# Two row transfers in flight, weights split early and kept, eight shared tiles behind the routed ones, sums on two engines

## The reference

```python
x = x + _L0_ffn_ref(_L0_cond_ref(x, ...), W_fc, W_proj)      # cosine attention, then a spiking FFN
x = x + _L1_ffn_ref(_L1_cond_ref(x, fside, ...), g1, g2, ...)  # attention, then a block with experts
...
# _L0_ffn_ref: h = square(relu(x @ W_fc.T)); y = h @ W_proj.T; 5 spiking steps on y; mean of the spikes
# _L1_ffn_ref:
X = X + attention(_rmsnorm(X, g1))
xf = _rmsnorm(X, g2)
rw = softmax(xf @ Wr.T + expert_bias)
topw, topi = top_k(rw, 2); topw = softmax(topw)
shared = _swiglu(xf, sW1, sW2, sW3)            # silu(x @ w1.T) * (x @ w3.T) @ w2.T
specialist = sum over the two chosen experts of topw * _swiglu(xf, eW1[e], eW2[e], eW3[e])
return X + shared + specialist
```

## Time and profile before

| what | value |
|---|---|
| three runs | 1443.07, 1442.61, 1438.27 us; median 1442.61 |
| the profiled execution | 1443.43 us, of it 1441.70 span from first to last instruction |
| granted TensorE clock, mean | 0.954 of full |
| busy, share of the span | PE 91%, VectorE 72%, ACT 62%, GpSimd 49% |
| moved | 71.19 MB, mean 49 GB/s |

### The profile page before, as it was taken

The page is one execution under the profiler, slowest core; times in us unless marked ns, Lnnn a source line. Parts: engine busy times, 40 slices in busy tenths (PEclk is TensorE's granted clock), DMA queues, the critical chain, the costliest instruction groups (busy, mean ns, idle before and its releaser), DMA issues.

```text
span 1441.7 us, 42824 instructions
## 1 busy us (share of the span) xinstructions
PE 1307.1 (91%) x15311; PEld 1157.7 (80%) x15312; DVE 1037.4 (72%) x2148; ACT 897.6 (62%) x2309; POOL 708.2 (49%) x797
## 2 busy tenths in 40 slices
PE   4899999999689999889999999689999789999980
PEld 3799999998579999778888888668788678888870
DVE  4798988988736465687887887768987686555446
ACT  3677777777356666656666666478775354555545
POOL 2556555564435454545445444357777562333330
PEclk8899999999799999999999999899997999999995
DMA  8200000001030000000000000020012623333319
GB/s 230 54 8 10 8 9 9 8 11 37 3 87 1 1 0 1 3 9 10 8 9 9 9 9 12 23 56 16 16 29 72 211 80 111 105 104 101 101 44 349
DMA packets 87025, 71.19 MB, mean 49 GB/s; under 512 B 49981, under 2 KB 80831, under 8 KB 85824
## 3 DMA queue, kind: packets, MB, share of 16 engines
q1 hardware_dynamic: 80320, 51.73, 12.7%
q0 software_dynamic: 6528, 17.05, 3.3%
HBM read 39.47 MB, written 24.02 MB: 44 GB/s over the span
## 4 chain that ended last, share of the span: by engine, by line
PE 56%; issue 20%; POOL 10%; DVE 9%; ACT 3%; DMA 1%; another core or an unknown queue 0%; ACTq 0%; POOLq 0%; DVEq 0%; SPq 0%
PE psQ L2348 9%; PE psQ L1957 7%; PE psW L2035 7%; PE psW L2327 5%; POOL pn L759 5%; PE psQ L2148 3%; POOL rq L785 3%; PE psS L2148 3%; PE psW L2136 3%; PE psM L2136 3%; PE psS L2059 2%; PE psT L1986 2%; PE psT L2070 2%; PE psM L2009 2%; PE psT L2316 2%
## 5 line engine op out<-in xcount | busy, mean ns | idle before, releaser
L1957 PE MATMUL psQ<-xT,wq 128*128 128x256 f32 x1536 | 224.8, 298 | 3.5 <-ACT cur L1117 1.8
L2035 PE MATMUL psW<-wout,oT 128*128 128x256 f32 x1536 | 207.8, 294 | 1.1 <-ACT oT L980 1.1
L1957 PEld LDWEIGHTS psQ<-xT,wq 128*128 128x128 f32 x1536 | 205.0, 201 | 4.4 <-issue 2.6
L2035 PEld LDWEIGHTS psW<-wout,oT 128*128 128x128 f32 x1536 | 196.6, 199 | 1.3 <-ACT oT L980 1.3
L2348 PE MATMUL psQ<-W,exT 128*128 (+1 forms) x624 | 172.3, 412 | 0.0
L759 POOL TENSOR_TENSOR pn<-ex,rden 128x1024 f32<-128x1024 f32 x64 | 124.5, 1945 | 45.2 <-DVE rden L1440 45.2
L980 ACT ACTIVATE oT<-psT,small 128x512 fp32r<-128x512 f32 x128 | 81.1, 684 | 91.3 <-PE psT L2070 91.2
L915 POOL DMA_INDIRECT results<-result,idx x72 | 70.1, 974 | 135.3 <-ACT result L1244 131.9
L803 POOL TENSOR_TENSOR hT<-hf,hT 128x512 fp32r<-128x512 f32 x64 | 85.8, 1341 | 102.1 <-ACT hT L1113 102.0
L771 POOL TENSOR_TENSOR masked_bias<-bias_t,negmask 128x1024 f32<-128x1024 f32 x32 | 68.8, 2150 | 132.6 <-DVE ex L1408 132.6
L1367 DVE SCALAR_TENSOR_TENSOR oT<-psT,small,oT 128x512 fp32r<-128x512 f32 x128 | 90.2, 746 | 58.3 <-ACT oT L980 58.3
(11 more groups left out here) (302 smaller groups left out, 3391.6 us busy)
## 6 DMA issues: line engine op xcount, KB each, us to landing
rows<-sorted SPq DMA_DIRECT2D x72, 132.0 KB, 2.1
both<-results SPq DMA_DIRECT2D x8, 1024.0 KB, 13.7
raw_w<-W SPq DMA_DIRECT2D x27, 256.0 KB
vv<-vp SPq DMA_DIRECT2D x256, 16.0 KB, 1.8
out<-X SPq DMA_DIRECT2D x8, 512.0 KB, 8.8
X<-x SPq DMA_DIRECT2D x1, 3584.0 KB, 18.1
bvv<-v_all SPq DMA_DIRECT2D x128, 16.0 KB
sorted<-rows SPq DMA_DIRECT2D x9, 132.0 KB
```

Of the source, the lines that this page charges most:

```text
L1957: mm = nc.tensor.matmul(psQ[:, cc, h * QT:h * QT + QT], wq[w][:, k, c * P:c * P + P], xT[g % 2][u][:, k, :], start=(k == 0 and j == 0), st ...
L2035: mm = nc.tensor.matmul(psW[:, 0:D], oT[u][:, c, :], wout[w][:, c, :], start=(u == 0 and c == 0 and w == 0), stop=(u == 1 and c == CH - 1))
```

## The change

- `FIRST` becomes 24: steps 0 to 23 are shared tiles, 24 to 95 the 72 routed tiles, 96 to 103 the last eight shared tiles.
- The raw pieces of the experts' weights are loaded during the FFN into three small buffers, both parts are made there by VectorE (3 pieces behind group 0, 4 behind each of groups 1 to 6), and SP stores each of the 27 pieces to a buffer in device memory (`parked`), waits for the store to land and loads the next but two piece. ACT and VectorE wait for the last store before they reuse the memory at the attention's start. Later an expert's weights come in as one load of 1.5 MB, already split: expert 0 at the end of the second attention (SP waits until it landed), then 1; 2 at the end of the block; 3 to 8 when the block's rows are done. ACT and VectorE do no splitting in the expert steps.
- Each send of rows waits until the send two before it has landed (`x_sent0`, `x_sent1`); the wait on PE's transpositions goes. The batches are (0, 8), (8, 24), (24, 32), 16 sends stand in the block, and the choices are cut into shorter parts at other steps.
- The experts' weights of the sum are computed in steps 9 to 21. ACT scales the results of groups 0 to 4 and VectorE sums groups 0 and 2 in steps 103 to 107; groups 1, 3 and 5 are summed by GpSimd, the others by VectorE behind the last step.

```diff
-FIRST = TILES
+FIRST = 3 * TILES // 4
-BATCHES = ((0, 12), (12, 24), (24, TILES))
-FIRST_CHOICE, SECOND_CHOICE, PLACES = (-14, -2, 5), (-13, -1, 6), (-11, 1, 8)
-RANKED_BEFORE, RANK = (19, 31), 7
-SEND_STEP, SENT_IN_BLOCK = 26, 14
-ENDS, SLOTS, MARGINS = (10, 12, 14), (16, 18, 20, 22, 24), 26
+BATCHES = ((0, 8), (8, 24), (24, TILES))
+FIRST_CHOICE, SECOND_CHOICE, PLACES = ((-18, -17), (-2, -2), (5, 5)), ((-16, -15), (-1, -1), (6, 6)), ((-12, -11), (2, 2), (8, 8))
+RANKED_BEFORE, RANK = 17, {2: 1, 7: 2}
+SEND_STEP, SENT_IN_BLOCK, IN_FLIGHT = 26, 16, 2
+ENDS, SLOTS, WEIGHTS = (10, 11, 12), (13, 14, 15, 16, 17), (9, 18, 20, 22)
+POOL_GROUPS = (1, 3, 5)
+SCALE_STEP, SUM_STEP = {103: 0, 104: 1, 105: 2, 106: 3, 107: 4}, {104: 0, 106: 2}
...
-SPLIT_STEP = [-4, -3, -2, 0, 1, 2, 3, 4, 5] + list(range(10, 28))
+PARKED = [3] + [4] * (GROUPS - 2)
+PIECES = KD + 1
...
+            def load_piece(n):
+                p, part = divmod(n, PIECES)
+                raw = raw_piece[n % 3][:, 1, :]
+                got = sem(f"p_raw{n % 3}")
+                if part < KD:
+                    for j, w in enumerate(("W1", "W3")):
+                        sp.dma_start(raw[:, j * D:j * D + D], a[w][p, part * P:part * P + P, :]).then_inc(got, 16)
+                else:
+                    sp.dma_start(raw.rearrange("p (k n) -> p k n", k=KD), a["W2"][p].rearrange("(k p) n -> p k n", p=P)).then_inc(got, 16)
+            def park(n):
+                p, part = divmod(n, PIECES)
+                sp.wait_ge(sem("p_lo"), n + 1)
+                sp.dma_start(parked[p, :, :, part * 2 * D:part * 2 * D + 2 * D], piece[n % 3][:].bitcast(F32)).then_inc(sem("p_kept"), 16)
+                sp.wait_ge(sem("p_kept"), 16 * (n + 1))
+            for n in range(3):
+                load_piece(n)
+            for n in range(PIECES * EP):
+                park(n)
+                if n + 3 < PIECES * EP:
+                    load_piece(n + 3)
             spread_v(LAYERS[1], load_block)
             def load_expert(p, slot, done):
...
+                sp.dma_start(W[:, slot, :, :].bitcast(F32), parked[p]).then_inc(done, 16)
             sp.wait_ge(sem("t_oev"), 2 * TILES)
-            for p in range(2):
-                load_expert(p, SHARED_SLOT + p, sem("e_first"))
+            load_expert(0, SHARED_SLOT, sem("e_weights"))
+            sp.wait_ge(sem("e_weights"), 16)
+            load_expert(1, SHARED_SLOT + 1, sem("e_weights"))
...
-                if n >= SENT_IN_BLOCK and k == 0:
-                    pool.wait_ge(sem("e_xTp"), (t - SENT_IN_BLOCK // TOP_K) * 8 // 7 + 1)
+                reach(pool, sem(f"x_sent{n % IN_FLIGHT}"), 16 * (n // IN_FLIGHT))
                 send(t, k)
...
+            for n, g in enumerate(POOL_GROUPS):
+                x = X[:, G4 * g:G4 * g + G4, :]
+                pool.wait_ge(sem("y_scaled"), g + 1)
+                nc.gpsimd.tensor_tensor(x, x, both[g][:, :, 0, :], ALU.add).then_inc(sem("y_half"), 1)
+                pool.wait_ge(sem("y_half"), 2 * n + 1)
+                nc.gpsimd.tensor_tensor(x, x, both[g][:, :, 1, :], ALU.add).then_inc(sem("y_half"), 1)
...
+            def split_piece(n):
+                part = n % PIECES
+                hi, lo = piece[n % 3][:, 0, :], piece[n % 3][:, 1, :]
+                raw = raw_piece[n % 3][:, 1, :]
+                dve.wait_ge(sem(f"p_raw{n % 3}"), (0 if n % 3 else 16) + sum(16 if m % PIECES == KD else 32 for m in range(n % 3, n + 1, 3)))
+                if part < KD:
+                    then(nc.vector.tensor_scalar(hi, raw, g2col[:, part:part + 1], None, ALU.mult))
+                    ins = nc.vector.scalar_tensor_tensor(lo, raw, g2col[:, part:part + 1], hi.bitcast(F32), ALU.mult, ALU.subtract)
+                else:
+                    then(nc.vector.tensor_copy(hi, raw))
+                    ins = nc.vector.tensor_tensor(lo, raw, hi.bitcast(F32), ALU.subtract)
+                ins.then_inc(sem("p_lo"), 1)
             ffn_in_lo(0, 0)
...
+            for g in range(GROUPS):
+                ffn(g, g % 2, first=g == 0, last=g == GROUPS - 1)
+                if g < GROUPS - 1:
+                    for n in range(sum(PARKED[:g]), sum(PARKED[:g + 1])):
+                        split_piece(n)
...
                     if isinstance(t, int) and t in (0, FIRST):
-                        pe.wait_ge(sem("e_wlo"), 3 * EP if t else 3)
+                        pe.wait_ge(sem("e_weights"), 16 * EP if t else 16)
```

More of the change, by code:

```diff
@@ L336, in build @@
         count = sb("ffn_work", "count", [P, G4 * D], BF16)
+        pieces_at = (place["xT"][0] - 8 * K, place["ffn_work"][0])
+        piece = [nc.alloc_sbuf_tensor_at(f"piece{i}", [P, 2, 2 * D], F32R, offset=pieces_at[i // 2] + 4 * K * (i % 2)) for i in range(3)]
+        raw_piece = [nc.alloc_sbuf_tensor_at(f"raw_piece{i}", [P, 2, 2 * D], F32, offset=pieces_at[i // 2] + 4 * K * (i % 2)) for i in range(3)]
         place["ffn_work"][0] += 8 * K
@@ L646, in _ @@
             sp.wait_ge(sem("d_xf"), TILES)
[L647 to L650, removed]
+            for p in range(3, EP):
+                load_expert(p, (p + 1) % EP, sem("e_weights"))
             def row_number(table, n, last):
@@ L662, in _ @@
             sp.wait_ge(sem("blanked"), 16 * (E + 1))
-            sp.wait_ge(sem("x_sent"), 16 * TOP_K * TILES)
+            for n in range(IN_FLIGHT):
+                sp.wait_ge(sem(f"x_sent{n}"), 16 * TOP_K * TILES // IN_FLIGHT)
             for r in range(ROUTED):
@@ L677, in _ @@
             for g in range(GROUPS):
-                sp.wait_ge(sem("y_acc"), g + 1)
+                done = sum(h not in POOL_GROUPS for h in range(g + 1))
+                if g in POOL_GROUPS:
+                    sp.wait_ge(sem("y_half"), 2 * (g + 1 - done))
+                else:
+                    sp.wait_ge(sem("y_acc"), done)
                 sp.dma_start(out_dram[:, G4 * g:G4 * g + G4, :], X[:, G4 * g:G4 * g + G4, :]).then_inc(sem("stored"), 16)
@@ L1804, in read_ranks, with places @@
                 dve.wait_ge(sem("r_read"), b + 1)
-            def places(b):
+            def places(b, k):
                 tiles = slice(*BATCHES[b])
-                if b == 2:
+                if b and k == 0:
                     read_ranks(b)
-                for k in range(TOP_K):
-                    mine = rt[1 + k][:, tiles, :]
-                    then(nc.vector.tensor_tensor(mine, mine, place_of[:, tiles, :], ALU.mult))
-                    then(nc.vector.tensor_reduce(pos[:, k, tiles], mine, AX.X, ALU.add))
+                mine = rt[1 + k][:, tiles, :]
+                then(nc.vector.tensor_tensor(mine, mine, place_of[:, tiles, :], ALU.mult))
+                then(nc.vector.tensor_reduce(pos[:, k, tiles], mine, AX.X, ALU.add))
+                if k == 0:
+                    return
                 nc.vector.tensor_copy(row_place[:, :, tiles], pos[:, :, tiles]).then_inc(sem("r_placed"), 1)
@@ L1896, in first_half @@
                     tile_slots(SLOTS.index(i))
-                elif i == MARGINS:
+                elif i == WEIGHTS[0]:
                     margins()
-                for piece in range(3 * EP):
-                    if SPLIT_STEP[piece] == i:
-                        split_expert(piece // 3, piece % 3)
+                if i == WEIGHTS[2] - 1:
+                    top_weights()
+                elif i == WEIGHTS[3] - 1:
+                    late_weights()
             def merged(i):
```

179 lines of the change are left out of this document (77 added, 102 removed).

## The result

The changed kernel takes 1476.91 us (median of 4 runs, 1474.19 to 1479.59) against 1441.69 for the kernel before (4 runs, 1438.27 to 1443.07): a ratio of 1.0249, interval 1.0229 to 1.0268. It is slower, by 2.5%. The forecast was 1462, range 1428 to 1482.

What follows compares the result with a forecast made beforehand. PE was taken to bound the FFN, with gains possible only in the shared steps and tail. The sum was 1443.4 + 25 + 2.5 + 2 - 11.5 + 1 = 1462.4, so 1462 us, range 1428 to 1482.

Steps and rivals of the forecast that it cites:

- FFN, +25: FFN: the fourth piece's wait for its reloaded buffer idles PE 3.3 us a group plus 1.7 of clock, five times.
- The transition, +2.5: Behind FFN group 6: four more pieces ahead of the next attention's norm_first cost 2.5 us, ends 0 and 5.
- The block's start, +2: Block's start: SP waits for the first expert's 1.5 MB before spreading bvv, costing 2 us, ends 0 and 4.
- The shared steps, -13.5 before the clock: Shared expert steps: rows let the first routed tile start at 1196 instead of 1209.8; -11.5 after the clock.
- The tail, +1: After the last routed product: 38.3 us against 37.5, ended by ACT's scalings, GpSimd's sums beside them; ends -3 and +4.
- The routed steps: Routed steps: the clock behind PE's wait for rows was put at 2 us, taken off the shared steps' gain.
- B: FFN rival: store and load are quick, so the kernel is not slower; centre 1436 us, chance 0.28.
- C: Expert-step rival: 48 sends in a row hold PE up, 7.1 us a gap; 1472 us, chance 0.15.
- D: Expert-step rival: sends keep their share beside the weights, landing 2.6, 9 us less, 1453; a quarter of the forecast's share.

Runs made afterwards that it cites:

- experiment 1: Changed kernel with two of the four weight pieces behind groups 1 to 6 moved ahead of ffn_in_lo, where VectorE is idle: 1456.16 us, ratio 1.0087.
- experiment 6: The run with both, experts 3 to 8 loaded one at a time: 1464.8 us; the last run of experiment 4 without SP's early wait for expert 0: 1451.72.
- Experiment 3: Changed kernel with all 32 shared tiles ahead of the routed ones again: 1471.21 us, ratio 1.0223.
- experiment 4: All eight result sums on VectorE, none on GpSimd: in the changed kernel 1474.21 us, in the run with both 1451.37.
- experiment 2: Changed kernel with four row sends in flight instead of two: 1466.44 us; with no limit on sends: 1486.07 us.
- the last run of experiment 4: The run with both, with all eight sums on VectorE and none on GpSimd: 1451.37 us, ratio 1.0075.
- experiment 5: Kernel before with only the limit of two sends in flight, in place of the wait on PE's transpositions: 1446.89 us, ratio 1.0045.
- the run with both: Changed kernel with weight pieces moved to VectorE's idle time and all 32 shared tiles ahead of the routed ones: 1454.6 us, ratio 1.01.

## Why the prediction was right, and where its terms were off

The direction and the main reason held, and the time lay 15 us under the measured one. That it came so near is in part luck. In the profiled execution two terms came out 28 us too low (the shared steps with the routed ones 22.7, the tail 5.7), and 16 of that were taken back: by the FFN's 4.8, and by 11.1 in the stretches outside it and ahead of the expert steps, where 4.5 were forecast and -6.6 measured, most of that spread. By its own steps:

- **FFN, +25: right in mechanism, 5 us too large.** Measured +20.2 in the FFN, and 20.7 undone by experiment 1. The fourth piece waits 2.4 to 2.7 us in each of six groups, PE stands 2.2 instead of 3.3 (store 3.2 where I put 3.6, load 2.2 where I put 2.6 with its issue), and the clock, 0.94 over 30 us, takes 1.8 more, where I put 1.7. Choosing 3.6 between 2.1 and 7.7 by the straight loads was the right choice of row.
- **The transition, +2.5: nothing.** From the last ffn_in_lo to the first product of the attention it is 31.2 as against 31.4.
- **The block's start, +2: PE did wait 3.25 us, yet the block got no longer.** From the first projection to the first expert step it takes 163.4 as against 165.5; by experiment 6 the wait cost some 1.5 of them.
- **The shared steps, -13.5 before the clock: this is the step that failed.** I wrote that two in flight hold the sends up only where a landing takes longer than 2 x 1.28, and the landing I took, 2.4, was right to the digit (2.43). But the next send doesn't start when the one before the last lands: it starts 0.8 us later, by the chain above. A pair takes 2.43 + 0.8 = 3.23, not 2.56. And beside the weights a landing took 6.0 to 7.3, not 4.0, which was the end of my range. With these, 8 sends in the 29 us from 1138 to 1167 and 1.61 for each of the 37 behind it, the first routed tile stands 109 behind the first step, not 87. So a term forecast as a gain was a loss of 8.1.
- **The tail, +1: +6.7.** I let ACT's scalings end it. VectorE's sums do: they start 13.7 us behind the last routed result instead of 8.3, because of the shared steps, and each of VectorE's steps that meets a sum of GpSimd lasts as long as that. I had counted GpSimd's 16 us as lying beside the rest. Experiment 3 shows 3 of it as the price of the eight tiles, experiment 4 a further 2.8 as that of the division.
- **The routed steps** took 3.1 more. Of it 2 are the clock, as I had put: it is half while PE waits (0.53 from 1188 to 1231) and 0.61 from 1231.4 to 1236.4, and full from there on. The other 1.1 are open.

Of the rivals, B falls with the store's 3.2 and the load's 2.2. C named the right time for the wrong reason: 48 sends in a row did come, but with two in flight no gap of PE came with them; experiment 2 shows that C's mechanism is real, and far larger than its price of 7.1 a gap, as soon as the pause behind each pair is gone. D, that the sends keep their share beside the weights, falls: landings of 6 to 7.3. The Trainium skill ("DMA: Bandwidth & Descriptors", section "SWDGE vs HWDGE vs iDMA") says that the two kinds of descriptors have queues of their own, between which each DMA engine takes turns. The runs agree in so far as the number of loads queued makes no difference (7.1 to 8.3 us a pair with one, 6.8 to 8.5 with six). Why a landing beside a load still takes 6 us and more, they don't show.

For VectorE beside GpSimd the Trainium skill ("GPSIMD Engine Reference", section "1. Specifications") says that the two share their interfaces to SBUF, so that a VectorE instruction with two inputs in SBUF contends with GpSimd. The trace agrees: L1952 reads two tensors of SBUF and took up to 2.57 beside GpSimd's 2.4 to 2.96, and 0.48 without it. It is about the length of a whole sum of GpSimd, and not a share of it.

The parts, by the traces: of the 31.4, the wait in the FFN is 20, the eight tiles behind the routed ones are 3 of the tail and the division of the sums a further 3. In the run with all three undone (the last run of experiment 4) the span is 1449.1, still 7.4 over the kernel before. The first routed transposition stands 110.8 behind the first expert step there (1102.3 to 1213.1), and 100.9 before: +9.9. The routed steps take 3.0 more and the tail 1.1, and 6.6 are gained ahead of the expert steps, most of it spread. Of the 9.9 the limit of two alone gives 4.6 (105.5 in experiment 5). The rest comes with the other changes of loading and sorting, which weren't tried singly. One of them can be seen: the split weights are twice the bytes (9.4 MB for six experts instead of 4.7), and the sends are slow for 27 us (1120 to 1147 in the run with both) where they were for 19 in experiment 5 (1119 to 1138).

What stays open: by which way the sends keep PE's signals from ACT and VectorE. The runs show that it takes sends with pauses of 0.30 us, with and without loads beside them, and that two in flight, with pauses of about 1 us behind each pair, end it. Whether the pause or the number in flight does that isn't told apart: three in flight and a fixed pause between the sends weren't tried.

## What to carry to other kernels

A wait on an in-order engine is priced by the whole round, and by everything queued behind it: store, landing, reload for a buffer, and landing plus the time to the next start for a limit on transfers in flight. Before such a wait is added, look for a place where the answer has long come: with two of each four pieces moved a few instructions ahead, the same 27 cost nothing. And a limit that seems to cost pace may protect something else; take it away on the chip before you call it a loss.

## What the runs showed of the hardware

- Indirect sends from GpSimd that follow each other with 0.30 us between them delayed what ACT and VectorE learn from PE, by up to 18.5 us (experiment 2, no limit) and 15.1 (four in flight); with two in flight and a pause of 0.95 behind each pair no such wait is seen.
- A VectorE instruction with two inputs in SBUF lasted 2.57 instead of 0.48 beside a GpSimd sum. So it is with the pieces in the FFN: the subtraction at 506.57 took 1.67 instead of 0.75, while GpSimd's ffn_lo ran from 506.37 to 507.69.
- A send of 132 KB lands in 2.43 us alone, in 6.0 to 7.7 beside a queue of six loads of 1.5 MB (changed kernel, run with both), and in 6.3 to 7.5 beside one at a time (experiment 6).
